# A Mamba-style hybrid layer on one core: 4-bit FFN weights decoded by shifts and a mask, with the decoded pieces turned between the first run's products

## The reference, cut to what matters

```python
_FP4_LUT = [0.0, 0.5, 1.0, 1.5, 2.0, 3.0, 4.0, 6.0, -0.0, -0.5, -1.0, -1.5, -2.0, -3.0, -4.0, -6.0]
def _dequant_fp4(packed_i32, scales_f16, group_size):      # 8 codes in each int32, low bits first
    nib = w[:, :, None] >> shifts & 15
    vals = _FP4_LUT[nib].reshape(out_f, in_p * 8)
    return vals * repeat(scales_f16.T, group_size, axis=1)  # one scale for 128 inputs of one output row
gate, up = split(layernorm(x) @ w_gu.T)                     # w_gu: 2*1408 x 512
y = (silu(gate) * up) @ w_down.T                            # w_down: 512 x 1408
x = x + y / sqrt(mean(y * y) + eps)
```

## Time and profile before

| | |
|---|---|
| median of three runs | 4797.97 us |
| the profiled execution | 4795.44 us |
| its span | 4793.6 us |
| TensorE busy over the span | 4570.4 us (95%) |
| VectorE busy | 3585.9 us (75%) |
| mean granted TensorE clock | 0.98 |
| head, first shift of a piece | 3434.62 us |
| first product of the second stage | 3676.53 us |

### The profile page before, as it was taken

How to read it: one execution, slowest core, us unless ns; L and a number is a source line. 1 busy time by engine, 2 the same in 40 slices (tenths; PEclk the granted TensorE clock), 3 DMA queues, 4 the chain that set the end, 5 groups by cost and what they waited for, 6 DMA issues and landing times. The chain is left out here.

```text
span 4793.6 us, 61029 instructions
## 1 busy us (share of the span) xinstructions
PE 4570.4 (95%) x20341; PEld 2909.4 (61%) x20341; DVE 3585.9 (75%) x8682; ACT 2307.5 (48%) x4841; POOL 514.6 (11%) x381
## 2 busy tenths in 40 slices
PE   7899999999999999999999999998577999999899
PEld 4677777677777677777677777667333444444343
DVE  5777777777777777777777777776475988988861
ACT  4455454555554555554554554553223554555433
POOL 1111111111111111111111111111010000000000
PEclk9999999999999999999999999999889999999999
DMA  2010110111100111100110100100200444444420
GB/s 75 31 34 32 35 33 27 34 32 29 38 30 27 34 33 58 43 29 27 34 34 27 38 29 27 34 27 10 83 1 18 161 144 136 156 145 145 150 90 18
DMA packets 202330, 262.10 MB, mean 55 GB/s; under 512 B 18174, under 2 KB 101378, under 8 KB 202018
## 3 DMA queue, kind: packets, MB, share of 16 engines
q1 hardware_dynamic: 202018, 258.20, 16.9%
HBM read 249.24 MB, written 8.91 MB: 54 GB/s over the span
## 5 line engine op out<-in xcount | busy, mean ns | idle before, releaser
L436 PE MATMUL bank<-xnT,w_qkv 128*128 128x512 f32 x2048 | 925.1, 594 | 4.1 <-ACT raw L720 3.4
L436 PEld LDWEIGHTS bank<-xnT,w_qkv 128*128 128x128 f32 x2048 | 373.5, 191 | 401.9 <-issue 383.2
L1004 DVE SCALAR_TENSOR_TENSOR conv<-raw,conv_w,conv 128x1024 f32<-128x1024 f32 x384 | 496.1, 1292 | 154.8 <-ACT conv L694 145.7
L547 PE MATMUL bank<-w_out_unit,oT 128*128 128x512 f32 x1024 | 497.1, 608 | 7.9 <-ACT oT L760 7.9
L508 PE MATMUL bank<-w_z_unit,xnT 128*128 128x256 f32 x2048 | 486.8, 381 | 0.0
L508 PEld LDWEIGHTS bank<-w_z_unit,xnT 128*128 128x128 f32 x2048 | 371.2, 191 | 41.2 <-issue 1.0
L791 ACT ACTIVATE squares<-o 128x128 f32<-128x128 f32 x512 | 153.9, 301 | 454.9 <-DVE o L1048 392.8
L1211 PE MATMUL bank<-xnT_f,w_gu 128*128 128x512 f32 x704 | 345.7, 637 | 11.1 <-PEq L1536 7.0
L1219 PE MATMUL bank<-xnT_f,w_gu 128*128 128x512 f32 x704 | 318.2, 595 | 0.0
L1229 PE MATMUL bank<-w_down,hidden 128*128 128x512 f32 x704 | 316.7, 593 | 1.1 <-DVE x_blocks L1271 1.1
L1103 POOL TENSOR_TENSOR inv<-n_base,block_mask 128x1024 f32<-128x1024 f32 x64 | 150.5, 2352 | 1422.2 <-DVE n_base L851 1422.2
(11 more groups left out here) (219 smaller groups left out, 8510.4 us busy)
## 6 DMA issues: line engine op xcount, KB each, us to landing
rows_b<-bc_rows SPq DMA_DIRECT2D x256, 256.0 KB, 3.3
rows_c<-bc_rows SPq DMA_DIRECT2D x256, 256.0 KB, 3.4
w_qkv<-in_w_qkv SPq DMA_DIRECT2D x128, 256.0 KB, 2.8
decay<-gc_rows SPq DMA_DIRECT2D x64, 512.0 KB, 3.9
w_z_unit<-in_w_z SPq DMA_DIRECT2D x32, 512.0 KB, 4.4
w_out_unit<-in_w_out SPq DMA_DIRECT2D x32, 512.0 KB, 5.0
x_after<-x SPq DMA_DIRECT2D x16, 256.0 KB, 2.0
x_blocks<-x_after SPq DMA_DIRECT2D x4, 1024.0 KB, 12.3
```

What stands on the lines that cost most here:

```text
L436: made = e.matmul(PROJ[:, :], w_qkv[:, p % 2, j, :], xnT[:, n // HK, j, h * BANK:(h + 1) * BANK], start=j == 0, stop=j == KT - 1)
L547: made = e.matmul(OB[:, :], oT[:, r, :], w_out[:, N % 2, r, :], start=r == 0, stop=r == REP - 1)
L1004: e.scalar_tensor_tensor(acc, raw[:, i % 2, tap:tap + T], conv_w[:, tap, col:col + 1], acc, ALU.mult, ALU.add).then_inc(on["conv"], 1)
```

## The change

Three things are changed, all in the head; the program of attention and the table of slots of the second stage are the same.

1. **Decoding.** A code is a sign, two bits of exponent and one of mantissa. A left shift brings it to the word's top, an arithmetic right shift by 6 brings exponent and mantissa to bits 24 to 22 of a float32 (the sign stays in bit 31), and one AND with `FLOAT_BITS` clears the rest. Read as float32 this is the value times 2^-126; the code for 0.5 is a denormal number. 2^63 is multiplied into the scales and again as a banked piece is evicted, both on ScalarE. `unpack` has 10 instructions where it had 15.
2. **Scaling.** VectorE multiplies by the scales, as `unpack`'s last instruction. GpSimd has no work left in the head; the tiles `mag` and `top` are gone.
3. **Order.** `beside(i, place)` gives the pieces of unit i+1 to places beside unit i: the first ahead of gate(i), the second between gate(i) and up(i), the others behind up(i). The state-space weights go two at a time behind the up products of units 2 to 6. ScalarE's evictions follow. The exponential of `rate` moves to i = 2 and its negation to i = 3.

```diff
+FLOAT_BITS = -0x7E400000
+HALF_POWER = 2.0 ** 63
-UNPACK_STEPS = NIB + 7
+UNPACK_STEPS = NIB + 2
...
+        def beside(i, place):
+            ahead = [("piece", k) for k in pieces_before(i + 1)] if i + 1 < IT else []
+            return (ahead[0:1], ahead[1:2], ahead[2:] + state_space[2 * (i - 2):2 * (i - 1)] if i >= 2 else ahead[2:])[place]
...
                 for i in range(IT):
-                    for k in pieces_before(i):
-                        prepare(("piece", k))
+                    for use in beside(i, 0):
+                        prepare(use)
                     e.wait_ge(on["prep_read"], prep_at[("piece", 2 * i)] + 1)
                     gate_mm(e, 0, i)
+                    for use in beside(i, 1):
+                        prepare(use)
                     e.wait_ge(on["prep_read"], prep_at[("piece", 2 * i + 1)] + 1)
                     up_mm(e, 0, i)
-                    if i == 0:
-                        for use in prep[prep_at[("small", 0)]:prep_at[("out_w", KT - 1)] + 1]:
-                            prepare(use)
-                    else:
+                    for use in beside(i, 2):
+                        prepare(use)
+                    if i > 0:
...
                         down_mm(e, 0, i - 1)
...
-                        made = e.copy(place, bank[:, 0:ng * P].rearrange("p (i w) -> p i w", w=P))
+                        made = e.mul(place, bank[:, 0:ng * P].rearrange("p (i w) -> p i w", w=P), HALF_POWER)
...
                     for j in range(NIB):
-                        e.tensor_scalar(spread[:, :, j], words, 4 * j, 15, ALU.logical_shift_right,
-                                        ALU.bitwise_and).then_inc(on["unpacked"], 1)
+                        e.tensor_scalar(spread[:, :, j], words, 4 * (NIB - 1 - j), 6, ALU.logical_shift_left,
+                                        ALU.arith_shift_right).then_inc(on["unpacked"], 1)
                     e.wait_ge(on["unpacked"], done + NIB)
-                    e.tensor_scalar(mg, nb, 7, None, ALU.bitwise_and).then_inc(on["unpacked"], 1)
+                    e.tensor_scalar(bits, bits, FLOAT_BITS, None, ALU.bitwise_and).then_inc(on["unpacked"], 1)
                     e.wait_ge(on["unpacked"], done + NIB + 1)
-                    e.tensor_scalar(vl, mg, -4.0, 0.0, ALU.add, ALU.max).then_inc(on["unpacked"], 1)
-                    e.tensor_scalar(tp, mg, 7.0, 2.0, ALU.is_ge, ALU.mult).then_inc(on["unpacked"], 1)
...
-                    e.tensor_tensor(vl, vl, tp, ALU.mult).then_inc(on["unpacked"], 1)
+                    e.tensor_tensor(values.rearrange("p (g w) -> p g w", g=ng),
+                                    bits.bitcast(F32).rearrange("p (g w) -> p g w", g=ng),
+                                    by.unsqueeze(2).broadcast_to([P, ng, P]), ALU.mult).then_inc(on["unpacked"], 1)
...
-            def gpsimd(e):
...
```

More of the change, by code:

```diff
@@ L1182 @@
     rows32 ffn_stats ffn_xn unpacked hidden residual ss_rate ss_stats ss_xn dt dtx drive scan c_mult pair_add out_add work_read
-    scaled
 """
@@ L1315, in second_half @@
         order = [k for i in range(IT) for k in pieces_before(i)]
+        state_space = [("small", 0), ("dt_rows", 0)]
+        state_space += [("dt_w", i) for i in range(KT)] + [("out_w", i) for i in range(KT)]
+        def beside(i, place):
+            ahead = [("piece", k) for k in pieces_before(i + 1)] if i + 1 < IT else []
+            return (ahead[0:1], ahead[1:2], ahead[2:] + state_space[2 * (i - 2):2 * (i - 1)] if i >= 2 else ahead[2:])[place]
         prep = [("scale", 0), ("scale", 1)] + [("turn0", t) for t in range(TILES)]
-        prep += [("piece", k) for k in pieces_before(0)] + [("small", 0), ("dt_rows", 0)]
-        prep += [("dt_w", i) for i in range(KT)] + [("out_w", i) for i in range(KT)]
-        prep += [("piece", k) for i in range(1, IT) for k in pieces_before(i)] + [("turn1", t) for t in range(TILES)]
+        prep += [("piece", k) for k in pieces_before(0)]
+        prep += [use for i in range(IT) for place in range(3) for use in beside(i, place)]
+        prep += [("turn1", t) for t in range(TILES)]
         prep_at = {use: k for k, use in enumerate(prep)}
@@ L1326, in second_half @@
             rows16, rows32, scale = hb("rows16", [P, 2, P], F16), hb("rows32", [P, 2, P]), hb("scale", [P, 2, P])
-            nib, mag = hb("nib", [P, 2, KT * P], I32), hb("mag", [P, 2, KT * P], I32)
-            val, top = hb("val", [P, 2, KT * P]), hb("top", [P, 2, KT * P])
+            nib, val = hb("nib", [P, 2, KT * P], I32), hb("val", [P, 2, KT * P])
             staged = {"dt_w": hb("dt_w", [P, KT, D]), "out_w": hb("out_w", [P, KT, D])}
@@ L1398, in prepare @@
                         ng = piece(i)[1]
-                        e.wait_ge(on["scaled"], order.index(i) + 1)
+                        e.wait_ge(on["unpacked"], UNPACK_STEPS * (order.index(i) + 1))
                         values = val[:, order.index(i) % 2, 0:ng * P].rearrange("p (g w) -> p g w", g=ng)
@@ L1406, in prepare @@
                     made.then_inc(on["prep_made"], 1)
-                for use in prep[:prep_at[("turn0", TILES - 1)] + 1]:
+                for use in prep[:prep_at[("piece", 1)] + 1]:
                     prepare(use)
                 for i in range(IT):
-                    for k in pieces_before(i):
-                        prepare(("piece", k))
+                    for use in beside(i, 0):
+                        prepare(use)
                     e.wait_ge(on["prep_read"], prep_at[("piece", 2 * i)] + 1)
                     gate_mm(e, 0, i)
+                    for use in beside(i, 1):
+                        prepare(use)
                     e.wait_ge(on["prep_read"], prep_at[("piece", 2 * i + 1)] + 1)
                     up_mm(e, 0, i)
-                    if i == 0:
-                        for use in prep[prep_at[("small", 0)]:prep_at[("out_w", KT - 1)] + 1]:
-                            prepare(use)
-                    else:
+                    for use in beside(i, 2):
+                        prepare(use)
+                    if i > 0:
                         if (i - 1) % KT == 0:
@@ L1436, in evict @@
                     if kind == "scale":
-                        made = e.copy(scale[:, i, 0:counts[i]], bank[:, 0:counts[i]])
+                        made = e.mul(scale[:, i, 0:counts[i]], bank[:, 0:counts[i]], HALF_POWER)
                     elif kind == "small":
@@ L1455, in scalar @@
                     evict(("turn0", t))
+                for k in pieces_before(0):
+                    evict(("piece", k))
                 for i in range(IT):
-                    for k in pieces_before(i):
-                        evict(("piece", k))
+                    for use in beside(i, 0):
+                        evict(use)
                     silu_gate(e, 0, i)
-                    if i == 0:
-                        for use in prep[prep_at[("small", 0)]:prep_at[("out_w", KT - 1)] + 1]:
-                            evict(use)
+                    if i == 2:
                         e.wait_ge(on["ss_params"], 48)
                         e.activation(rate[:, :, :], rate[:, :, :], ACT.Exp).then_inc(on["rate_exp"], 1)
+                    for place in (1, 2):
+                        for use in beside(i, place):
+                            evict(use)
                     if i == IT - 2:
@@ L1472, in unpack @@
                 def unpack(k):
-                    words, ng, _, _ = piece(k)
+                    words, ng, by, _ = piece(k)
                     at = order.index(k)
-                    nb, mg, vl, tp = (t[:, at % 2, 0:ng * P] for t in (nib, mag, val, top))
-                    spread = nb.rearrange("p (w j) -> p w j", j=NIB)
+                    bits = nib[:, at % 2, 0:ng * P]
+                    spread = bits.rearrange("p (w j) -> p w j", j=NIB)
+                    values = val[:, at % 2, 0:ng * P]
                     done = UNPACK_STEPS * at
@@ L1482, in unpack @@
                         e.wait_ge(on["words"], 32)
+                    if at == 0:
+                        e.wait_ge(on["prep_read"], 2)
                     for j in range(NIB):
[L1484 to L1485 removed]
+                        e.tensor_scalar(spread[:, :, j], words, 4 * (NIB - 1 - j), 6, ALU.logical_shift_left,
+                                        ALU.arith_shift_right).then_inc(on["unpacked"], 1)
                     e.wait_ge(on["unpacked"], done + NIB)
[L1487 removed]
+                    e.tensor_scalar(bits, bits, FLOAT_BITS, None, ALU.bitwise_and).then_inc(on["unpacked"], 1)
                     e.wait_ge(on["unpacked"], done + NIB + 1)
[L1489 to L1498 removed]
+                    e.tensor_tensor(values.rearrange("p (g w) -> p g w", g=ng),
+                                    bits.bitcast(F32).rearrange("p (g w) -> p g w", g=ng),
+                                    by.unsqueeze(2).broadcast_to([P, ng, P]), ALU.mult).then_inc(on["unpacked"], 1)
                 e.wait_ge(on["scale_rows"], 32)
@@ L1514, in vector @@
```

(3 more changed lines are left out.)

## The result

The changed kernel takes 4714.99 us (median of four runs, 4711.11 to 4719.19) against 4795.33 us for the kernel before in the same comparison. The ratio is 0.9832, with a 95% interval from 0.9815 to 0.9849: 80 us faster. Predicted were 4718 us, with a range of 4707 to 4740. The profiled execution took 4716.24 us; the sum had given 4716.1.

What follows compares the result with a forecast made beforehand. VectorE's decoding was taken to bound the head, TensorE after the change. Unit times and small waits put the head's last turns at 3584.4 instead of 3663.68, 79.3 us earlier: 4716.1 profiled, 4718 us predicted, range 4707 to 4740.

Steps and rivals of the forecast that it cites:

- the sum: Step times added through the head from the first shift at 3434.62, giving 4716.1 us for the profiled execution.
- The bound before and after: In the head, VectorE's decoding chain bounds before; TensorE bounds after, at 11.61 us a unit against VectorE's 6.7.
- A piece's price: VectorE's decoding of one piece in the head: shifts 0.97, AND 0.46, scales product 0.61, together 2.04 us, before 5.48.
- The first two units: Start of the head: TensorE idles for most of 8 us before gate(1), taken as 5.83 us; unit 1 ends at 3473.7.
- The units: Units 2 to 8 of the head: 11.61 us each on TensorE, 1.35 us more in units 3 to 6.
- The wait behind the statistics: Ahead of unit 9, VectorE takes statistics first, 2.74 us; less 0.70 of cover, TensorE waits 2.0 us.
- The tail: Last turns, down(10), squares and residual at the head's end: same instructions as before, 12.85 us.
- The head as a whole: From the first shift to the second stage's first product, expected near 3597: 162.6 us summed.
- The first, a clock that stays low: Rival: in the head TensorE's clock does not rise or the cover is too thin, 4731 or 4741 us; 17 in 100.
- The second, the third piece and the hidden product holding each other: Rival: TensorE's wait stays once a unit of the head, gain mostly lost, 4736 up to 4765 us; 4 in 100.
- The third, slower: Rival: the head's new shift pair or denormal-reading product leaves the fast path, 4888 us; 2 in 100.
- a cover of 0.70 us: At a unit's first piece, VectorE's chain of 3.17 us runs beside 3.87 us of TensorE work, leaving 0.70 us.

Runs made afterwards that it cites:

- the two half changes: Against the kernel before: the new decoding with the old order of pieces, 4730.5 us; the new order with the old decoding, 4779.94 us.
- the added instructions: The changed kernel with more full-width VectorE instructions in each piece, results unused: three more, 4741.09 us; one more, 4721.88 us in one run.
- the first trace of before: First profiled execution of the unchanged kernel, on which the prediction was based: 4795.44 us, first shift at 3434.62, second stage 1117.1 us.
- its two repeats: The unchanged kernel profiled twice more: 4793.65 and 4794.69 us, one run each; first shift at 3438.77 and 3439.86, head 239.8 us in both.

## Why the prediction was right

**The bound before and after.** Right. VectorE was the chain, TensorE took over, and the two half changes and the added instructions show it from either side.

**A piece's price.** Right to a hundredth of a microsecond. The first piece of the changed kernel:

```profile
3439.40 0.93 DVE L1502 TENSOR_SCALAR nib<-words_gu 128x64 int32<-128x64 int32 x8
3440.37 0.43 DVE L1505 TENSOR_SCALAR nib<-nib 128x512 int32<-128x512 int32 x1
3440.83 0.69 DVE L1507 TENSOR_TENSOR val<-nib,scale 128x512 f32<-128x512 f32 x1
3441.44 0.94 DVE L1502 TENSOR_SCALAR nib<-words_gu 128x64 int32<-128x64 int32 x8
```

The pitch is 2.04 us, as summed. The new pair of shifts costs what the old did (0.93 us for eight), the AND with a 32-bit constant what the AND with 7 did (0.43), and the broadcast of the scales nothing (0.69). Denormal inputs leave the product at 0.69 us; the codes are drawn at random, so about one in eight is 0.5 or -0.5, a denormal number here. By the Trainium skill, "VectorE: DVE Perf Modes", section "The DRAIN you can't avoid", the prediction estimated about 2.8 us a piece. That took only the section's first rule; the same section adds that a next instruction that is not held starts earlier. The measured 0.93 us for eight shifts, each recorded with about 0.22 us, agree with the addition and not with eight full durations.

**The first two units.** The sum gave 39.1 us from the first shift to the end of unit 1, that is of down(0); it took 38.3 us (3439.40 to 3477.74). The idle stretches were where they were counted:

```profile
3452.84 3.60 PE L1221 MATMUL bank<-xnT_f,w_gu 128*128 128x512 f32 x8
...
3456.27 1.04 PE L1411 MATMUL bank<-ident,val 128*128 128x128 f32 x8
3459.18 0.63 PE L1411 MATMUL bank<-ident,val 128*128 128x128 f32 x4 [1.87 <-DVE nib L1502]
3461.22 0.77 PE L1411 MATMUL bank<-ident,val 128*128 128x128 f32 x4 [1.41 <-DVE val L1507]
3463.86 1.08 PE L1411 MATMUL bank<-ident,val 128*128 128x128 f32 x4 [1.87 <-DVE nib L1502]
3464.74 5.42 PE L1213 MATMUL bank<-xnT_f,w_gu 128*128 128x512 f32 x8
```

Most of the difference is the clock of gate(1), 5.25 us to the next turns instead of the 5.83 assumed. Such a product took between 4.51 and 6.19 us behind an idle stretch in these traces, so no row of before gives it closer than that.

**The units.** Unit 2 took 12.72 us (predicted 12.56), unit 3 12.96 (12.96). The wait behind the statistics was predicted as 2.0 us. The profile shows 1.84 us of idle time; counted as the sum counts, from start to start, it is 5.43 less 3.43, so 2.00 us:

```profile
3561.45 3.60 PE L1231 MATMUL bank<-w_down,hidden 128*128 128x512 f32 x8
3566.88 0.63 PE L1411 MATMUL bank<-ident,val 128*128 128x128 f32 x4 [1.84 <-DVE nib L1502]
...
3588.39 0.60 PE L1307 MATMUL bank<-ident,xn_f 128*128 128x128 f32 x4
...
3601.24 1.19 PE L1213 MATMUL bank<-xnT_f,w_gu 128*128 128x512 f32 x1 [7.02 <-PEq L1536]
```

The tail is 12.85 us, to the hundredth what it was the earlier trace rows. The head as a whole: 162.6 us summed, 161.8 measured.

**Where luck helped.** The total fits better than the argument deserves. The sum took over from one trace the start of the head and the length of the second stage. In the profiled execution the head began 4.8 us later than in that trace and the second stage was 3.9 us shorter; with the 0.8 us that the head took less than its sum, the three cancel. The first two come from the first trace of before, as its two repeats show. I had given the change 79.3 us; against those repeats the head gained 78.0.

**The rivals.** The first, a clock that stays low, holds only for gate(0) and gate(1), which the sum had priced; from unit 2 on every gate product takes 3.60 us. But the argument against it was too easy: it asked for waits as long as the old ones, and a single wait of 2.56 us, in the kernel with one more instruction a piece, already had a slow gate product behind it. The wait of the changed kernel, 1.84 us, was not far from that. The second, the third piece and the hidden product holding each other, describes the old order, and the kernel with the new decoding in that order shows its price: 13.9 us of waits, less than the 18 to 47 us that I had given it. The third, slower, did not come: the shifts kept their 0.93 us and the product its 0.69.

## What to carry to other kernels

When a chain moves from one engine to another, price the new bound with its own program: sum the products of one unit, then follow the one hand-over that cannot run ahead and compare it with what covers it. Here that gave a cover of 0.70 us; adding some 0.7 us a piece left no wait in the units 2 to 8, and adding 2.17 us left 1.45. Once the other engine is the bound, relieving the old one further (GpSimd's multiply) is worth little, 1.9 us by the rows and nothing that the times can tell, while two more buffers for the values, where the pipeline starts up, took some 6 us off the head (158.7 to 152.6, one trace each). And look at how waits are spread: three stretches with 3.25 us in all, with a product between them, left TensorE's clock up, where a single one of 2.56 us had a slow product behind it.

## What the runs showed of the hardware

- TensorE's clock can stay up through short waits with products between them. In the kernel with the new order and the old decoding, three idle stretches of 0.40 to 1.43 us in a unit of 16.7 us leave the gate product at 3.60 us for eight matmuls. Behind single stretches of 1.84, 1.87 and 2.32 us the gate product took 3.60, behind 2.56 us 5.16, behind 4.01 us 5.29, behind 5.59 us 6.19. The 2.32 us are those behind the statistics in the kernel that scales on GpSimd.
- These pairs are no price list. In one trace of the kernel before (its first repeat) two waits of 4.63 us have gate products of 6.18 and 4.64 us behind them:

```profile
3604.20 0.87 PE L1402 MATMUL bank<-ident,val 128*128 128x128 f32 x3 [4.63 <-POOL val L1533]
3604.87 6.18 PE L1211 MATMUL bank<-xnT_f,w_gu 128*128 128x512 f32 x8
...
3641.44 0.88 PE L1402 MATMUL bank<-ident,val 128*128 128x128 f32 x3 [4.63 <-POOL val L1533]
3642.11 4.64 PE L1211 MATMUL bank<-xnT_f,w_gu 128*128 128x512 f32 x8
```

- Short waits with little between them did not keep the clock. Ahead of gate(1) of the changed kernel stand waits of 1.87, 1.41 and 1.87 us with one piece's turns between them, and gate(1) takes 5.42 us (lines above). No run here changes the length of a wait alone.
- A VectorE product that reads denormal float32 numbers takes no longer than another (0.69 us for 128x512), and an arithmetic shift behind a left shift in one instruction takes what a right shift with an AND takes (0.93 us for eight of 128x64).
- A GpSimd product of 1.07 us slows the eight VectorE shifts beside it from 0.93 to 1.78 us in the kernel with GpSimd's scaling, and to 1.79 us in the one before.
- Parts of the program that no change touched moved by several microseconds from one trace to the next, the first shift between 3434.62 and 3443.73 us and the length of the second stage between 1111.1 and 1117.9, so a single trace is no ground for a difference of a few microseconds outside the edited part.
